# Exponential of the attention scores in two halves of 512 columns, each with its own signal

## The reference

```python
q, k, v = (proj(wq), proj(wk), proj(wv))          # (b, 16, 2048, 128)
q, k = apply_rope(q, k, sin, cos)
att = jnp.einsum('bhqd,bhkd->bhqk', q, k) * (1.0 / math.sqrt(HD))
att = jax.nn.softmax(att, axis=-1)
y = jnp.einsum('bhqk,bhkd->bhqd', att, v)
...
x = _layernorm(x + attn(x, wq, wk, wv, wo))
x = _layernorm(x + ffn(x, wq_gate, s_gate, wq_up, s_up, wq_down, s_down))
```

## Time and profile before

| | us |
|---|---|
| median of 3 runs | 4780.23 |
| lowest and highest of them | 4529.89, 4853.41 |
| the profiled execution | 4529.02 |
| its span on core 4, the slowest | 4527.2 |
| spans of the 8 cores | 4513.4 to 4527.2 |
| attention in it, from the first score matmul on | 752 to 2165 |

### The profile page before, as it was taken

The page is one execution under the profiler, slowest core; times in us unless marked ns, Lnnn a source line. Parts: engine busy times, 40 slices in busy tenths (PEclk is TensorE's granted clock), DMA queues, the critical chain, the costliest instruction groups (busy, mean ns, idle before and its releaser), DMA issues.

```text
span 4527.2 us, 41877 instructions; the slowest of 8 cores (4513.4 to 4527.2 us)
## 1 busy us (share of the span) xinstructions
PE 3832.6 (85%) x15680; PEld 1493.8 (33%) x15680; DVE 608.4 (13%) x1312; ACT 1308.6 (29%) x1061; POOL 358.1 (8%) x680
## 2 busy tenths in 40 slices
PE   4999998777777777777994999998983999999982
PEld 1444443111111111111441444443431444444431
DVE  0222100000000110000221100001212000011112
ACT  0111112334433333433342333330005333330004
POOL 1000000000000000000000000002220000002220
PEclk8999998888888888888996999999997999999996
DMA  7333331010001001100366334436564544434553
GB/s 133 61 68 96 83 75 43 14 29 14 14 15 28 15 14 22 21 15 5 121 191 149 75 75 78 80 62 92 71 124 108 103 78 80 76 70 54 71 115 109
DMA packets 200710, 310.94 MB, mean 69 GB/s; under 512 B 99265, under 2 KB 152642, under 8 KB 191682
## 3 DMA queue, kind: packets, MB, share of 16 engines
q0 software_dynamic: 97344, 188.85, 25.3%
q1 hardware_dynamic: 98562, 115.22, 8.4%
q10 hardware_dynamic: 4608, 4.20, 0.3%
HBM read 412.86 MB, written 58.72 MB: 104 GB/s over the span
## 4 chain that ended last, share of the span: by engine, by line
PE 76%; DMA 11%; ACT 5%; DVE 4%; issue 4%; SPq 0%; DVEq 0%; POOL 0%; ACTq 0%; POOLq 0%
PE PS L601 13%; PE PS L594 13%; PE PS L485 10%; PE PS L615 9%; PE PS L537 6%; PE PS L533 6%; PE PS L570 5%; PE PS L500 5%; DMA AB<-wd_c 5%; PE PS L522 4%; ACT AB L660 3%; PE PS L525 3%; DMA AB<-AB 3%; DMA AB<-xT 2%; PE PS L544 1%
## 5 line engine op out<-in xcount | busy, mean ns | idle before, releaser
L660 ACT ACTIVATE AB<-PS,AB 128x1024 bf16<-128x1024 f32 x512 | 563.4, 1112 | 854.4 <-PE PS L525 854.3
L594 PE MATMUL PS<-AB 128*128 128x512 bf16 x2816 | 634.5, 383 | 123.0 <-ACT AB L726 55.5
L615 PE MATMUL PS<-AB 128*128 128x512 bf16 x2816 | 630.4, 386 | 74.3 <-DVE AB L825 74.2
L601 PE MATMUL PS<-AB 128*128 128x512 bf16 x2816 | 623.4, 380 | 0.0
L485 PE MATMUL PS<-AB 128*128 128x512 bf16 x2048 | 449.4, 383 | 61.9 <-DMA AB<-xT 61.9
L522 PE MATMUL PS<-AB 128*128 128x512 bf16 x512 | 246.9, 482 | 294.9 <-DVE AB L772 280.5
L594 PEld LDWEIGHTS PS<-AB 128*128 128x128 bf16 x2816 | 275.6, 98 | 467.6 <-issue 141.7
L533 PE MATMUL PS<-AB 128*128 128x512 bf16 x896 | 393.5, 439 | 36.1 <-ACT AB L660 36.1
L615 PEld LDWEIGHTS PS<-AB 128*128 128x128 bf16 x2816 | 276.0, 99 | 428.8 <-issue 119.0
L601 PEld LDWEIGHTS PS<-AB 128*128 128x128 bf16 x2816 | 275.7, 98 | 333.7 <-issue 2.2
L537 PE MATMUL PS<-AB 128*1 128x512 bf16 x896 | 377.3, 421 | 0.0
(11 more groups left out here) (76 smaller groups left out, 1696.8 us busy)
## 6 DMA issues: line engine op xcount, KB each, us to landing
AB<-wg_c POOLq DMA_DIRECT2D x88, 512.0 KB, 5.0
AB<-wu_c POOLq DMA_DIRECT2D x88, 512.0 KB, 7.0
AB<-wd_c POOLq DMA_DIRECT2D x352, 128.0 KB, 2.9
AB<-x SPq DMA_DIRECT2D x16, 1024.0 KB, 5.7
x1f<-AB SPq DMA_DIRECT2D x16, 1024.0 KB, 4.0
AB<-x1f SPq DMA_DIRECT2D x16, 1024.0 KB, 5.7
out<-AB SPq DMA_DIRECT2D x16, 1024.0 KB, 6.1
AB<-xT POOLq DMA_DIRECT2D x16, 512.0 KB, 13.3
```

Of the source, the lines that this page charges most:

```text
L594: mm = t.matmul(bank(par * 4 + cch)[:, 0:512], GDQ[par][:, di * 128:(di + 1) * 128], X1T[:, di * 1024 + cch * 512: di * 1024 + (cch + 1) * ...
L601: mm = t.matmul(bank(par * 4 + 2 + cch)[:, 0:512], UDQ[par][:, di * 128:(di + 1) * 128], X1T[:, di * 1024 + cch * 512: di * 1024 + (cch + ...
L615: mm = t.matmul(bank(tt)[:, 0:512], HT[:, h2 * 1024 + tt * 128: h2 * 1024 + (tt + 1) * 128], WDQ[i % 4][:, 0:512], start=(h2 == 0), stop=( ...
L660: sc.activation(PT[u % 4], bank(2 * (u % 2), 2)[:, 0:1024], AF.Exp, bias=CVC[:, 0:1], scale=ASCL).then_inc(s2sc, 1)
```

## The change

The exponential of a unit is done by two instructions of 512 columns, one for each key tile, and each raises `s2sc`. The semaphore therefore counts to 16 in a chunk where it counted to 8, and PE's waits for it are rewritten: the waits ahead of the scores still ask for both halves of the unit two before, and the wait ahead of the values moves into the loop over the two key tiles, so that the first value matmul waits for the first half and the second for the second. The values of the last unit of a chunk are treated alike. `s2st` is still raised once, by the second score matmul.

```diff
                     if u >= 2:
-                        t.wait_ge(s2sc, 8 * m + u - 1)
+                        t.wait_ge(s2sc, 2 * (8 * m + u - 1))
                     elif m >= 1:
-                        t.wait_ge(s2sc, 8 * (m - 1) + 7 + (1 if u == 1 else 0))
+                        t.wait_ge(s2sc, 2 * (8 * (m - 1) + 7 + (1 if u == 1 else 0)))
...
-                        t.wait_ge(s2sc, 8 * m + up + 1)
                         for kk in (2 * up, 2 * up + 1):
+                            t.wait_ge(s2sc, 2 * (8 * m + up) + (kk % 2) + 1)
...
-                t.wait_ge(s2sc, 8 * m + 8)
                 for kk in (14, 15):
+                    t.wait_ge(s2sc, 2 * (8 * m + 7) + (kk % 2) + 1)
...
-                    sc.activation(PT[u % 4], bank(2 * (u % 2), 2)[:, 0:1024],
+                    sc.activation(PT[u % 4][:, 0:512], bank(2 * (u % 2))[:, 0:512],
+                                  AF.Exp, bias=CVC[:, 0:1],
+                                  scale=ASCL).then_inc(s2sc, 1)
+                    sc.activation(PT[u % 4][:, 512:1024], bank(2 * (u % 2) + 1)[:, 0:512],
                                   AF.Exp, bias=CVC[:, 0:1],
                                   scale=ASCL).then_inc(s2sc, 1)
```

## The result

Over 10 runs the changed kernel's median is 4488.82 us (4419.91 to 4945.27), and that of the kernel before is 4801.88 us (4529.89 to 5081.19). The ratio of the changed kernel to the one before is 0.978, with a 95% interval of 0.969 to 0.987: 2.2% faster, where 0.976 was forecast.

A forecast was written before the change was run, and what follows sets the result against it. PE was taken as the bound, with idle waits and a lower granted clock in attention. 62 chunks x (22.19 - 20.48) = 106 us, plus some 1 us, off 4529.0 gave 4422 us; range 14 us downward, upward to 4495.

The forecast's parts named there:

- End of a chunk: Last unit's values: L544 no longer waits for the whole exponential and starts 0.32 us earlier in each chunk.
- The mechanism behind the gain: Attention: closing most of PE's idle time at each chunk's start brings the clock's rise earlier; 22.19 to 20.48 us a chunk.
- The price of a half: ACT: an exponential of 512 columns takes 0.686 us, where the whole one takes 1.112.
- ACT's load: ACT in attention: 512 more instructions, 82 us of work, all beside PE; 1.17 us of cadence in a 1.69 us unit.
- rival D: ACT: a half exponential costs nearly a whole one, ACT becomes the bound, 170 us come on top: 4700 us; chance 0.03.
- The added wait: PE ahead of the second value matmul, 512 times: costs nothing, at most 0.15 us each.
- Start of a chunk: First value matmul L533 starts 0.43 us earlier, 0.13 us of idle time stays; worth 0.25 us a chunk.
- The clock: Attention's granted clock: long low stretches shrink from 10.24 to 6.83 us, chunks from 22.19 to 20.48; 106 us over 62 chunks.
- the hole: PE's 0.56 us idle time between a chunk's first scores and first values, expected to delay the clock's rise.
- The sum for attention: Attention stage: 106 us over 62 chunks and some 1 us from the first two, 107 us less.
- rival A: Attention: idle time closes but the clock doesn't follow; 0.57 us a chunk, 36 us, 4493 us; chance 0.18.
- the 0.41 us for each us at the lower clock: Attention after PE's restart: 2.24 us more at the lower clock cost 0.92 us, taken from two neighbouring chunks.

The follow-up runs named there:

- e6: The kernel before with only the exponential of unit 7 of each chunk split; no ratio, 22.07 us a chunk on core 4 against 22.09.
- e4: The kernel before with the change's 512 waits added ahead of the second value matmul, exponentials whole; no ratio, attention 1391.6 us against 1391.7.
- e1: The kernel before plus one surplus score matmul in each chunk, between the second score pair and the first value matmul; ratio 0.980, 20.67 us a chunk.
- e2: The changed kernel with the first value matmul of each chunk waiting for both halves of unit 0; ratio 1.000, 22.08 us a chunk.
- e5: The kernel before with only the exponential of unit 0 of each chunk split; ratio 0.976, 20.38 us a chunk.
- e10: The kernel before with 20 surplus matmuls in each handover, where PE waits between chunks; ratio 0.966, attention 143.5 us shorter.
- e3: The changed kernel with every value matmul pair waiting for both halves of the exponential; no ratio, 22.66 us a chunk.

## What was right in the prediction, and the steps that failed

Two steps of the sum failed. Its base, the profiled execution's 4529.0 us, isn't the kernel's time, and *End of a chunk*, 0.32 us a chunk "all of it on the path", or 20 us in the stage, is worth 4.7 in the mean of the cores (e6). The mechanism behind the gain was right.

Step by step: *The price of a half:* 0.686 us forecast, 0.687 and 0.681 measured. *ACT's load:* steady units still take 1.69 us, and ACT stands idle in them for 0.42, so rival D falls. *The added wait:* forecast nothing, and e4 shows 1391.6 us against 1391.7. *Start of a chunk:* L533 was to start at 2.00 us after the restart with 0.13 of the idle time left; it is 2.00, and 0.14. *The clock:* low stretches of 6.83 us only and 20.48 us a chunk were forecast, with a rise 4.2 us after the restart and a fall 2.7 before; in the rows above the rise is 3.96 after and the fall (1008.21) 2.87 before. One reading was wrong, though nothing rests on it: "nearly all" of the chain is PE, but the shares in the earlier trace rows add up to 75% for PE, 10% for DMA and 3% for ACT. That the hole was the cause, which the prediction could only take from two chunks, is shown from both sides, by e1, which fills it and gains 89.5 us in the stage, and by e2, which opens it again and loses all. The sum for attention, 107 us, measured 107.1. The Trainium skill's sentence that the warm-up is a budget of time and not of a number of matmuls (TensorE: Matmul & The Clock Gate, What's actually happening) stood in the prediction for rival A. Read as a fixed delay after the first matmul it doesn't agree with e1, where with one more matmul behind the restart the rise comes 3.22 us after it, and in the kernel before 5.63 and 7.87.

The absolute number was off. The 4422 us were taken from the profiled execution of 4529.0, and the prediction set them beside the lowest run and forecast of the median only the ratio; as a time they are met by four of the ten runs of the changed kernel, 4419.91 to 4427.64, and not by its median, 4488.82, and held against the median of the kernel before, 4801.88, they would be 7.9% less where 2.2% was measured. The step that failed is the last one of the sum, in which the profiled execution's 4529.0 us stood for the kernel's time: what the runs show in its place is a median of 4801.88 before and a ratio of 0.978, and a forecast in terms of the median would have been 0.976 of that. The mechanism has no part in this.

Two terms were mis-sized. *End of a chunk* claimed 0.32 us "all of it on the path". Locally it is there (L544's wait is gone), but e6 has 1.6 us in the whole stage on core 4, and 4.7 in the mean of the cores, and not 20; and e5 has the whole gain without it. While the clock repeats its pattern, a chunk's length is set by that pattern, and what is saved elsewhere goes into a longer time at 1.2 GHz. That the sum for attention still came out to a tenth of a us isn't to the credit of these terms: the chunk of 20.48 us was taken from the clock's pattern, 6.83 and 13.65, and the direct gains only served to see whether it could hold. So the forecast's split of 1.71 us a chunk into 0.57 direct and 1.14 of the clock doesn't describe parts that can be had one by one. And the 0.41 us for each us at the lower clock, taken between two neighbouring chunks, was too much for the whole stage: e10 gives 143.5 us where it gives 180.

What stays open: how much of a hole after the restart the rise tolerates. The runs have only holes of about 0.14 us (the change, and what is left of it in e1), 0.56 and 0.71. Open too is why the saving at the end of a chunk gives 1.6 us on one core of e6 and 10.3 on another.

## What to carry to other kernels

Where PE stops for some us in each round of a loop, read the granted clock by stretches before adding up waits: a hole of half a us shortly after a restart can cost several times its length, because the rise comes later, and a saving elsewhere in the round can be worth next to nothing. A cheap test is to put a surplus matmul into the hole: if the kernel gets faster by more work, the clock was the price. The larger gain lay in the stop itself, not in its echo: taking the handover off the path gave 10% with the split, and the split was then worth its plain 0.7 us a chunk.

## What the hardware showed that was not expected

- Surplus matmuls made the kernel faster: 64 of them in the hole by 2% (e1), 1240 in the handovers by 3.4% (e10, ratio 0.966).
- The loop and the granted clock held each other in a nearly fixed pattern. On core 4, four kernels with different waits (before, e2, e4, e6) have chunks of 22.07 to 22.09 us, and two (the changed one and e5) 20.39 and 20.38. Only e1, with 20.67, and e3, with 22.66, lie apart.
- At 2.4 GHz the wait for ACT at the start of a chunk is longer, 62.2 us in e10 against 36.1: what runs before the wait gets faster, and the exponential doesn't (1.112 us before, 1.113 in e10).
